# Block 15 sums its products of Q and state in TensorE's transposes, GpSimd makes four of its rows of K times v, and the calls of all engines are in another order

## The chip, the cores and the metric

The kernel runs on one core of one Trainium2 chip. Its time is the device time of one launch in microseconds (us). The kernel before has a median of 511.01 us over three runs (510.86 to 511.65).

## The reference

The input x is 8 sequences of 1024 tokens of 128 features, all float32. One layer is computed: a gated linear recurrence with 16 heads of width 8, then a normalisation, then a feed-forward part of hidden width 512 and a second normalisation. Cut to what matters:

```
q, k, v = x @ Wq, x @ Wk, x @ Wv                 # heads of 8
f = sigmoid(x @ Wf + bf)
state[i, j] = state[i, j] * f[i] + v[i] * k[j]   # for every token, per head
out[i] = sum over j of state[i, j] * q[j]
out = (layernorm(out) * gamma + beta) * silu(x @ Wg)
x1 = layernorm(x + out @ Wout)
h = silu(x1 @ w1 * s1) * (x1 @ w2 * s2)
h = gelu(h @ h1 * sh1);  h = gelu(h @ h2 * sh2)
y = layernorm(x1 + (h @ w3) * s3)
```

## The kernel before, in words

The 8192 tokens are cut into 16 blocks of 512. Every block has the same work, block 0 and the last feed-forward part in forms of their own. Two blocks make one sequence, so the state starts at zero in even blocks and is carried over in odd ones.

**Recurrence.** Features lie on the 128 partitions, tokens along the row. TensorE makes v, f, k, q and the gate from xT (project_v and so on). q and k go out to a buffer in memory and come back so that each of 8 rows j holds, on all partitions of a head, feature j of k (tile KJ) or of q (tile QJ). For each j, K times v is formed, then a scan over the 512 tokens with the forget gate g (scan, L1601). DVE forms K times v two rows at a time (kv, L1585), rows 0 to 5 in most blocks; GpSimd forms rows 6 and 7 one at a time (kv_gp, L550). DVE multiplies Q by the state two rows at a time (qs, L1608). The sum over the 8 rows is then made by three adds of two rows each on DVE (add, L1616), which leave two rows, and one add of one row on GpSimd (add_gp, L556). sum_transposed (L2313) transposes the one row left in 4 chunks of 128 tokens into PSUM bank back. The blocks in the set EARLY, before only block 1, do it otherwise: GpSimd makes rows 4 to 7 of K times v, no adds are done, and sum_transposed accumulates the 8 rows in 32 transposes.

**Rest of the attention.** Statistics on DVE (stats_o), their root on GpSimd (rstd_of), the norm on ScalarE (norm_o), a transpose (transpose_y), scale and shift on ScalarE (affine), the gate on GpSimd (gated_y), the output product (attention_out), the residual on DVE, the statistics and norm of x1, and its transpose (transpose_x1), which ScalarE splits into a high part and DVE into a low part (x1_lo).

**Feed-forward part.** The products run in fp32r, with activations as high plus low part. up_hi and up_lo give the two up-projections in four groups t; ScalarE applies silu and DVE multiplies (hmul, L1665). Two middle layers follow, each with mid_open, mid_hi and mid_lo: the low parts come from GpSimd (lo, L489) and gelu from ScalarE. last_begin and last_rest make the last product and residual_2 adds x1. Block 15's feed-forward part is cut into two halves (tail_ calls).

**Order.** Nothing schedules at run time: each engine has one list of calls written out by hand, and semaphores tie the lists together. TensorE overwrites a PSUM bank only behind the wait that a table FREED names. sum_transposed(n) waits for the sum (in EARLY blocks for all products of Q and state, qs_done) and for residual_2(n-2), which reads bank back. In rest(), up_hi(n, t) with t of 2 or 3 waits for hmul of t-2, and mid_open of layer 1 waits for three hmul at t = 0 and for all four at t = 2. For a while at the start TensorE is given products that nobody reads (keep_busy, L2242). The weights' low parts are summed at the start and a flag tells TensorE which of two program parts to run: count_low_parts (L2485) on TensorE, set_flag (L1724) on DVE, then the load of the flag and a branch.

Of the kernel before, what the change touches and what calls it, by code (L numbers as in the profile page):

```python
# [3 lines left out]
def build_program(nc, x_d, xT_d, wproj_d, wffn_d, w3_d, w3s_d, cols_d, ident_d, out_d):  # L4
# [22 lines left out]
    EARLY = range(1, 2)  # L27
# [10 lines left out]
    with ctx:  # L38
# [213 lines left out]
        def _(e):  # L252
# [84 lines left out]
            send(1, 1)  # L337
            load_w3()
            load_xT(3)
            fetch(1, 1, 0)  # L340
            fetch(1, 1, 1)
            send(1, 0)
            load_weights(3)
            load_x(0)
# [9 lines left out]
            load_x(1)  # L354
            send(3, 0)
            fetch(2, 0, 1)
            fetch(3, 1, 0)
            fetch(3, 1, 1)
            send(4, 1)
            load_x(2)  # L360
            load_x(3)
            load_xT(5)
            fetch(3, 0, 0)
            load_x(4)
            fetch(4, 1, 0)
            load_x(5)
            fetch(3, 0, 1)
            send(4, 0)
            fetch(4, 1, 1)
            fetch(4, 0, 0)  # L370
            fetch(4, 0, 1)
            send(5, 1)
            load_xT(6)
            store(0)
            fetch(5, 1, 0)
            fetch(5, 1, 1)
            send(5, 0)
            fetch(5, 0, 0)
            fetch(5, 0, 1)
            send(6, 1)  # L380
            load_xT(7)
            load_xT(8)
            load_x(6)
            fetch(6, 1, 0)
            fetch(6, 1, 1)
            store(1)
            send(6, 0)
            fetch(6, 0, 0)
            load_xT(9)
            fetch(6, 0, 1)  # L390
            store(2)
            send(7, 1)
            load_x(7)
            load_xT(10)
            send(7, 0)
            fetch(7, 1, 0)
            fetch(7, 1, 1)
            send(8, 1)
            load_x(8)
            fetch(7, 0, 0)  # L400
# [3 lines left out]
            send(8, 0)  # L404
            fetch(8, 0, 0)
            fetch(8, 1, 1)
            load_x(9)
            send(9, 1)
            load_xT(11)
            fetch(8, 0, 1)  # L410
            send(10, 1)
            load_x(10)
            fetch(9, 1, 0)
            send(9, 0)
# [3 lines left out]
            load_xT(12)  # L418
            load_x(11)
            fetch(9, 0, 1)  # L420
            send(10, 0)
            fetch(10, 1, 0)
            fetch(10, 0, 0)
            store(5)
            send(11, 1)
            fetch(10, 0, 1)
            fetch(10, 1, 1)
            fetch(11, 1, 0)
            fetch(11, 1, 1)
            send(11, 0)  # L430
            load_xT(13)
            fetch(11, 0, 0)
            fetch(11, 0, 1)
            store(6)
            send(12, 0)
            load_x(12)
            load_x(13)
            load_xT(14)
            send(12, 1)
            fetch(12, 1, 0)  # L440
            fetch(12, 0, 0)
            store(7)
            fetch(12, 0, 1)
            send(13, 0)
            fetch(12, 1, 1)
            fetch(13, 0, 0)
            send(13, 1)
            load_x(14)
            store(8)
            fetch(13, 1, 0)  # L450
            fetch(13, 1, 1)
            store(9)
            fetch(13, 0, 1)
            load_xT(15)
            send(14, 1)
            fetch(14, 1, 0)
            load_x(15)
            send(14, 0)
            fetch(14, 1, 1)
            send(15, 1)  # L460
            fetch(14, 0, 0)
            fetch(15, 1, 0)
            store(10)
            fetch(14, 0, 1)
            fetch(15, 1, 1)
            send(15, 0)
# [4 lines left out]
            store(13)  # L471
            store_last(1)
            store(14)
# [9 lines left out]
        def _(e):  # L483
# [87 lines left out]
            kvj_gp(4)  # L571
            scale_w3()
            qsj_gp(1)
# [6 lines left out]
            kv_gp(1, 6)  # L580
            rstd_of(0, "1")
            kv_gp(1, 7)
# [19 lines left out]
            lo(1, 1, 2)  # L602
            lo(1, 1, 3)
            gated_y(2)
            rstd_2(0)
            lo(2, 1, 0)
            lo(2, 1, 1)
            rstd_of(2, "1")
            lo(2, 1, 2)
            lo(2, 1, 3)  # L610
            kv_gp(4, 6)
            add_gp(3)
            lo(1, 2, 0)
            lo(1, 2, 1)
# [2636 lines left out]
```

## Time and profile before

| | us |
|---|---|
| median of the runs | 511.01 |
| the profiled execution | 511.23 |
| its span | 509.4 |
| TensorE (PE) busy | 495.7 |
| VectorE (DVE) busy | 447.6 |
| ScalarE (ACT) busy | 404.9 |
| GpSimd (POOL) busy | 311.0 |

The span runs from the first to the last instruction in the trace. Busy times are sums over the span; a matmul's record covers its latency, so a PE that is shown busy can still hold small gaps between the starts of two matmuls. PEld is the loading of weights, which runs beside the matmuls.

### The profile page before, as it was taken

The numbers are of one execution on the slowest core, as the hardware profiler recorded it, in microseconds if no ns is written. First come the engines' busy times: TensorE is split into PE (matmuls) and PEld (weight loads), VectorE is DVE, ScalarE is ACT, GpSimd is POOL, SyncE is SP. The second block draws the span as 40 slices with busy tenths as digits, with TensorE's granted clock in tenths as the row PEclk, the third lists the DMA queues.
The fourth block names the chain that finished last, engine by engine and source line by source line (L and its number), as shares of the span: only waits on it lengthen the run. The fifth ranks groups of instructions, "written<-read, shape, count | busy, mean of one in ns | idle before, by whom it ended". The sixth has DMA issues, their size and how long they took to land. (4 is left out here: it accounts for less than half of the span.)

```text
span 509.4 us, 7961 instructions
## 1 busy us (share of the span) xinstructions
PE 495.7 (97%) x2528; PEld 383.1 (75%) x2528; DVE 447.6 (88%) x708; ACT 404.9 (79%) x839; POOL 311.0 (61%) x362
## 2 busy tenths in 40 slices
PE   9989999999999999999999999999999999999995
PEld 5667787777877777777877777777877777777895
DVE  3999999999989999999899999899999899992352
ACT  5765878787888977888897887889878788868764
POOL 0742839577592838768384775848385784929341
PEclk9999999999999999999999999999999999999999
DMA  7997999935797779768988895905875850700001
GB/s 244 250 269 181 258 257 226 234 87 150 186 264 195 221 178 239 187 164 201 248 210 214 209 257 150 244 2 145 209 181 154 218 126 18 190 1 1 23 2 65
DMA packets 21772, 87.33 MB, mean 171 GB/s; under 512 B 2528, under 2 KB 3552, under 8 KB 13792
## 3 DMA queue, kind: packets, MB, share of 16 engines
q1 hardware_dynamic: 21440, 86.46, 66.9%
q8 instruction: 22, 0.36, 0.3%
q10 hardware_dynamic: 288, 0.33, 0.2%
q14 instruction: 22, 0.18, 0.1%
HBM read 74.72 MB, written 12.06 MB: 170 GB/s over the span
## 5 line engine op out<-in xcount | busy, mean ns | idle before, releaser
L915 ACT ACTIVATE h<-F,cols 128x512 f32<-128x512 f32 x120 | 80.4, 688 | 11.3 <-PE F L2345 10.6
L489 POOL TENSOR_TENSOR h1lo<-h,h1hi 128x512 fp32r<-128x512 f32 x60 | 76.2, 1289 | 11.9 <-ACT h1hi L908 11.8
L489 POOL TENSOR_TENSOR h2lo<-h,h2hi 128x512 fp32r<-128x512 f32 x60 | 76.0, 1288 | 6.7 <-ACT h2hi L908 6.6
L1601 DVE TENSOR_TENSOR_SCAN KJ<-g,carry,KJ 128x512 f32<-128x512 f32 x64 | 78.2, 1262 | 0.0
L2345 PE MATMUL F<-h2hi,whi 128*128 128x512 f32 (+1 forms) x256 | 74.7, 424 | 0.2
L1601 DVE TENSOR_TENSOR_SCAN KJ<-g,KJ 128x512 f32<-128x512 f32 x64 | 74.3, 1203 | 0.7 <-POOL KJ L537 0.4
L1608 DVE TENSOR_TENSOR QJ<-QJ,KJ 128x1024 f32<-128x1024 f32 x60 | 71.2, 1213 | 0.2
L2345 PE MATMUL F<-h1hi,whi 128*128 128x512 f32 (+1 forms) x256 | 68.9, 411 | 2.4 <-DVE h L1665 2.1
L550 POOL TENSOR_TENSOR KJ<-KJ,v_sb 128x512 f32<-128x512 f32 x32 | 42.4, 1332 | 43.9 <-DMA KJ<-qk_bounce 26.9
L2345 PE MATMUL F<-h1lo,whi 128*128 128x512 f32 (+1 forms) x256 | 67.1, 401 | 0.0
L2345 PE MATMUL F<-h2lo,whi 128*128 128x512 f32 (+1 forms) x256 | 65.8, 398 | 0.4 <-POOL h2lo L489 0.3
L2246 PE MATMUL front<-xT,wproj 128*128 128x512 f32 x122 | 63.1, 598 | 0.8 <-ACT gate L855 0.6
L556 POOL TENSOR_TENSOR QJ<-QJ 128x512 f32<-128x512 f32 x14 | 18.0, 1285 | 74.1 <-DVE QJ L1616 74.1
L2345 PEld LDWEIGHTS F<-h1hi,whi 128*128 128x128 f32 x256 | 44.9, 188 | 22.9 <-issue 11.6
L2345 PEld LDWEIGHTS F<-h2hi,whi 128*128 128x128 f32 x256 | 46.9, 188 | 19.9 <-issue 6.7
L2446 PEld LDWEIGHTS back<-w,h 128*128 128x128 f32 x480 | 57.5, 191 | 2.7 <-DVE x1lo L1660 0.5
L2446 PE MATMUL back<-w,h 128*128 128x128 f32 x480 | 58.2, 275 | 0.0
L2345 PEld LDWEIGHTS F<-h1lo,whi 128*128 128x128 f32 x256 | 46.2, 188 | 12.4 <-issue 2.9
L2345 PEld LDWEIGHTS F<-h2lo,whi 128*128 128x128 f32 x256 | 45.7, 188 | 12.2 <-POOL h2lo L489 2.0
L1616 DVE TENSOR_TENSOR QJ<-QJ 128x1024 f32<-128x1024 f32 x42 | 52.3, 1245 | 1.3
L1585 DVE TENSOR_TENSOR KJ<-ps_v,KJ 128x1024 f32<-128x1024 f32 x44 | 52.7, 1207 | 0.0
L902 ACT ACTIVATE h<-F,cols 128x512 f32<-128x512 f32 x60 | 40.0, 685 | 14.3 <-PE F L2345 13.7
(183 smaller groups left out, 934.9 us busy)
## 6 DMA issues: line engine op xcount, KB each, us to landing
KJ<-qk_bounce SPq DMA_DIRECT2D x30, 1024.0 KB, 9.9
QJ<-qk_bounce SPq DMA_DIRECT2D x30, 1024.0 KB, 10.7
qk_bounce<-qk SPq DMA_DIRECT2D x30, 256.0 KB, 4.0
x_in<-in_x SPq DMA_DIRECT2D x16, 256.0 KB, 9.1
xT<-in_xT SPq DMA_DIRECT2D x15, 256.0 KB, 4.9
out<-res SPq DMA_DIRECT2D x15, 256.0 KB, 5.8
wraw<-in_wffn SPq DMA_DIRECT2D x2, 1024.0 KB, 9.4
wraw<-in_wffn SPq DMA_DIRECT2D x2, 256.0 KB, 4.7
```

The lines of the kernel that those rows point to most:

```text
L489: e.tensor_tensor(h_lo[layer][:, t, :w], h[:, t, :w], h_hi[layer][:, t, :w].bitcast(f32), ALU.subtract).then_inc(lo_done[layer], 1)
L550: e.tensor_tensor(K, K, v_sb[:, :WIDTH[n]], ALU.mult).then_inc(kv_gp_done, 1)
L556: e.tensor_tensor(first, first, other, ALU.add).then_inc(add_gp_done, 1)
L902: e.activation(h[:, t, :WIDTH[n]], F[2 * (t % 2)][:, :WIDTH[n]], ACT.Silu, scale=S1[t]).then_inc(silu_done, 1)
L915: e.activation(dst[:, t, :WIDTH[n]], F[t][:, :WIDTH[n]], ACT.Gelu, scale=scale[t]).then_inc(gelu_done[layer], 1)
L1585: e.tensor_tensor(K, vb, K, ALU.mult).then_inc(kv_done, 1)
L1601: e.tensor_tensor_scan(K, g[:, :WIDTH[n]], K, init, ALU.mult, ALU.add).then_inc(scan_done, 1)
L1608: e.tensor_tensor(Q, Q, rows(KJ, n)[:, 2 * p:2 * p + 2, :], ALU.mult).then_inc(qs_done, 1)
L1616: e.tensor_tensor(first, first, other, ALU.add).then_inc(add_done, 1)
L2246: return e.matmul(bank[:, :WIDTH[n]], weights, xT[n % XTB][:, :WIDTH[n]], start=True, stop=True)
L2345: return e.matmul(out, whi[:, cs], part, start=start, stop=stop)
L2446: return e.matmul(back[:, chunk(c)], h3[:, k, chunk(c)], w3[:, k, :], start=k == 0, stop=k == NH - 1)
```

## The change

Block 15 joins the set EARLY. With that, its sum goes into 32 transposes, its three adds on DVE and its add on GpSimd are gone, DVE forms rows 0 to 3 of K times v and GpSimd rows 4 to 7. The functions read this from EARLY. One function gets a wait (save_carry, for the order of two writes of the same tile). All else is order: the lists of SP, GpSimd, ScalarE, DVE and TensorE are written anew, and the table FREED with them.

```diff
-    EARLY = range(1, 2)
+
+    EARLY = (1, 15)
...
             def save_carry(n):
+                if n:
+                    e.wait_ge(carry_done, n)
                 e.wait_ge(scan_done, HD * (n + 1))
...
             kv_gp(14, 7)
-            rstd_of(13, "1")
             lo(2, 12, 1)
             lo(2, 12, 2)
             lo(2, 12, 3)
+            rstd_of(13, "1")
+            add_gp(14)
             rstd_2(11)
-            add_gp(14)
-            kv_gp(15, 6)
             lo(1, 13, 0)
+            lo(1, 13, 1)
             rstd_of(14, "o")
-            lo(1, 13, 1)
+            kv_gp(15, 4)
             lo(1, 13, 2)
             lo(1, 13, 3)
             gated_y(14)
-            kv_gp(15, 7)
+            kv_gp(15, 5)
             lo(2, 13, 0)
             lo(2, 13, 1)
+            rstd_of(14, "1")
             lo(2, 13, 2)
-            rstd_of(14, "1")
             lo(2, 13, 3)
-            add_gp(15)
+            kv_gp(15, 6)
+            kv_gp(15, 7)
             lo(1, 14, 0)
+            rstd_2(12)
+            lo(1, 14, 1)
             rstd_of(15, "o")
-            lo(1, 14, 1)
             lo(1, 14, 2)
+            rstd_2(13)
             lo(1, 14, 3)
             gated_y(15)
-            rstd_2(12)
             lo(2, 14, 0)
             lo(2, 14, 1)
             rstd_of(15, "1")
             lo(2, 14, 2)
             lo(2, 14, 3)
-            rstd_2(13)
```

The first place is the end of DVE's part in block 15. KJ1 and QJ1 are the block's rows, h<-F1 and h<-F3 are the hmul of block 14. Before:

```order
L1585 TENSOR_TENSOR KJ1<-ps_v,KJ1 128x1024
L1601 SCALAR_TENSOR_TENSOR KJ1<-g,carry,KJ1 128x512
L1655 TENSOR_TENSOR x_in2<-back,x_in2 128x512
L1601 SCALAR_TENSOR_TENSOR KJ1<-g,carry,KJ1 128x512
L1620 BN_STATS stats_1<-x_in2 128x6 x4
L1626 BN_AGGR mv_1<-stats_1 128x2 x4
L1601 SCALAR_TENSOR_TENSOR KJ1<-g,carry,KJ1 128x512 x3
L1608 TENSOR_TENSOR QJ1<-QJ1,KJ1 128x1024 x3
L1660 TENSOR_TENSOR x1lo<-back,x1hi 128x512
L1616 TENSOR_TENSOR QJ1<-QJ1 128x1024
L1608 TENSOR_TENSOR QJ1<-QJ1,KJ1 128x1024
L1616 TENSOR_TENSOR QJ1<-QJ1 128x1024 x2
```

And now the same stretch:

```order
L1659 TENSOR_TENSOR x_in2<-back,x_in2 128x512
L1624 BN_STATS stats_1<-x_in2 128x6 x4
L1630 BN_AGGR mv_1<-stats_1 128x2 x4
L1605 SCALAR_TENSOR_TENSOR KJ1<-g,carry,KJ1 128x512 x3
L1664 TENSOR_TENSOR x1lo<-back,x1hi 128x512
L1605 SCALAR_TENSOR_TENSOR KJ1<-g,carry,KJ1 128x512 x2
L1612 TENSOR_TENSOR QJ1<-QJ1,KJ1 128x1024 x3
L1669 SCALAR_TENSOR_TENSOR h<-F1,cols,h 128x512
L1612 TENSOR_TENSOR QJ1<-QJ1,KJ1 128x1024
L1677 TENSOR_TENSOR res1<-back,x1_1 128x512
L1669 SCALAR_TENSOR_TENSOR h<-F3,cols,h 128x512
```

The adds are gone, x1lo moved ahead of the last two scans, and the first hmul moved ahead of the fourth product of Q and state.

The second place is GpSimd around block 15's rows. KJ1<-KJ1,v_sb is a row of K times v, h1lo and h2lo are low parts of block 13. Before:

```order
L550 TENSOR_TENSOR KJ1<-KJ1,v_sb 128x512
L489 TENSOR_TENSOR h1lo<-h,h1hi 128x512
L518 TENSOR_TENSOR rstd_o<-mv_o,eps4 128x4
...
L489 TENSOR_TENSOR h1lo<-h,h1hi 128x512 x3
L562 TENSOR_TENSOR y<-y,gate2 128x512
L550 TENSOR_TENSOR KJ1<-KJ1,v_sb 128x512
L489 TENSOR_TENSOR h2lo<-h,h2hi 128x512 x3
L518 TENSOR_TENSOR rstd_1<-mv_1,eps4 128x4
...
L489 TENSOR_TENSOR h2lo<-h,h2hi 128x512
L556 TENSOR_TENSOR QJ1<-QJ1 128x512
```

And now:

```order
L551 TENSOR_TENSOR KJ1<-KJ1,v_sb 128x512
L490 TENSOR_TENSOR h1lo<-h,h1hi 128x512 x2
L563 TENSOR_TENSOR y<-y,gate2 128x512
L551 TENSOR_TENSOR KJ1<-KJ1,v_sb 128x512
L490 TENSOR_TENSOR h2lo<-h,h2hi 128x512 x2
L519 TENSOR_TENSOR rstd_1<-mv_1,eps4 128x4
...
L490 TENSOR_TENSOR h2lo<-h,h2hi 128x512 x2
L551 TENSOR_TENSOR KJ1<-KJ1,v_sb 128x512 x2
L490 TENSOR_TENSOR h1lo<-h,h1hi 128x512
```

The row that stood ahead of the low parts now stands in their midst, and the last two rows follow all of block 13's low parts.

The third place is TensorE ahead of the branch. The tile F<-ones_col,low_any is count_low_parts, F<-wproj,ident is keep_busy, back<-ident,x_0 is transpose_x1(0). Before:

```order
L2331 MATMUL back<-wproj,y 128x128 x4
L2242 MATMUL F<-wproj,ident 128x128 x10
L2485 MATMUL F<-ones_col,low_any 1x1 x4
L2246 MATMUL front<-xT,wproj 128x512
L2242 MATMUL F<-wproj,ident 128x128 x16
L2230 MATMUL back<-ident,x_0 128x128 x4
L2246 MATMUL front<-xT,wproj 128x512
L2242 MATMUL F<-wproj,ident 128x128
L3205 TENSOR_LOAD flag
```

And now:

```order
L2246 MATMUL ps_v<-xT,wproj 128x512
L2246 MATMUL front<-xT,wproj 128x512
L2331 MATMUL back<-wproj,y 128x128 x4
L2242 MATMUL F<-wproj,ident 128x128 x26
L2230 MATMUL back<-ident,x_0 128x128 x4
L2485 MATMUL F<-ones_col,low_any 1x1 x4
L2242 MATMUL F<-wproj,ident 128x128
L2246 MATMUL front<-xT,wproj 128x512
L3205 TENSOR_LOAD flag
```

The count moved behind transpose_x1(0), the projections moved around it; on DVE, set_flag moved from ahead of half_norm("1") to behind qs(1, 0) and qs(1, 1).

## Rows read from the trace of the kernel before

**Rows 1.** The page: busy time of each engine, and the clock line.

```profile
PE 495.7 (97%) x2528; PEld 383.1 (75%) x2528; DVE 447.6 (88%) x708; ACT 404.9 (79%) x839; POOL 311.0 (61%) x362
...
PEclk9999999999999999999999999999999999999999
```

**Rows 2.** Windows, all engines: stretch, length, busy us and instructions, clock, DMA share, GB/s.

```profile
60.00:420.00 360.00, 357.40 (x1744) 273.72 (x1743) 341.99 (x508) 299.54 (x621) 239.22 (x273) 1.00 0.77 192
420.00:460.00 40.00, 37.83 (x199) 29.57 (x197) 38.89 (x60) 30.98 (x60) 21.68 (x25) 1.00 0.27 67
460.00:509.40 49.40, 43.50 (x304) 39.42 (x302) 15.82 (x58) 33.91 (x82) 22.94 (x31) 0.98 0.07 23
```

**Rows 3.** Waits of PE: us in total, times, longest.

```profile
PE F L2345 <- DVE h L1665: 2.8, 5, 1.1
```

**Rows 4.** Timeline of PE at block 1's sum: start, us, engine, line.

```profile
49.07 3.65 PE L2313 MATMUL back<-ident,QJ 128*128 128x128 f32 x32
```

**Rows 5.** Timelines of PE and PEld around block 15's sum.

```profile
456.89 0.60 PE L2313 MATMUL back<-ident,QJ 128*128 128x128 f32 x4
...
459.62 3.17 PE L2345 MATMUL F<-h1hi,whi 128*128 128x512 f32 x12 [1.14 <-DVE h L1665]
...
455.86 0.30 PEld L2345 LDWEIGHTS F<-x1hi,whi 128*128 128x128 f32 x2 [0.58 <-DVE h L1665]
...
460.18 2.16 PEld L2345 LDWEIGHTS F<-h1hi,whi 128*128 128x128 f32 x10 [0.30 <-DVE h L1665]
```

**Rows 6.** Sources, one line each: ns min/median/max, first and last start.

```profile
L1616 DVE TENSOR_TENSOR QJ<-QJ x42: 1214/1219/2250, 70.7 to 453.9; 128x1024 f32<-128x1024 f32 x42
...
L1585 DVE TENSOR_TENSOR KJ<-ps_v,KJ x44: 1190/1212/1218, 24.5 to 437.6; 128x1024 f32<-128x1024 f32 x44
...
L556 POOL TENSOR_TENSOR QJ<-QJ x14: 1272/1282/1304, 76.1 to 455.2; 128x512 f32<-128x512 f32 x14
...
L550 POOL TENSOR_TENSOR KJ<-KJ,v_sb x32: 1262/1288/2176, 26.8 to 437.2; 128x512 f32<-128x512 f32 x32
...
L902 ACT ACTIVATE h<-F,cols x60: 672/687/691, 44.9 to 458.5; 128x512 f32<-128x512 f32 x60
```

**Rows 7.** Timeline of DVE, end of block 15's part.

```profile
442.82 3.60 DVE L1601 TENSOR_TENSOR_SCAN KJ<-g,carry,KJ 128x512 f32<-128x512 f32 x3
446.34 3.47 DVE L1608 TENSOR_TENSOR QJ<-QJ,KJ 128x1024 f32<-128x1024 f32 x3
...
455.06 0.75 DVE L1665 SCALAR_TENSOR_TENSOR h<-F,cols,h 128x512 f32<-128x512 f32 x1
```

**Rows 8.** Timeline of POOL, 427 to 446 us.

```profile
428.18 1.28 POOL L550 TENSOR_TENSOR KJ<-KJ,v_sb 128x512 f32<-128x512 f32 x1
...
439.05 2.53 POOL L489 TENSOR_TENSOR h2lo<-h,h2hi 128x512 fp32r<-128x512 f32 x2 [0.52 <-ACT h2hi L908]
441.81 1.28 POOL L489 TENSOR_TENSOR h2lo<-h,h2hi 128x512 fp32r<-128x512 f32 x1 [0.23 <-ACT h2hi L908]
...
444.58 1.30 POOL L489 TENSOR_TENSOR h2lo<-h,h2hi 128x512 fp32r<-128x512 f32 x1
```

**Rows 9.** Timelines at the branch: DVE, PE; the flag's load by its source line.

```profile
40.58 0.12 DVE L1724 CAST flag<-F 1x1 int32<-1x1 f32 x1
...
41.14 2.34 DVE L1608 TENSOR_TENSOR QJ<-QJ,KJ 128x1024 f32<-128x1024 f32 x2
...
46.32 1.39 DVE L1665 SCALAR_TENSOR_TENSOR h<-F,cols,h 128x512 f32<-128x512 f32 x2
...
43.50 0.71 PE L2345 MATMUL F<-x1hi,whi 128*128 128x512 f32 x2
...
L3205 PEldq TENSOR_LOAD <-flag x1: 489/489/489, 41.6 to 41.6; - x1
```

**Rows 10.** Timelines of DVE and ACT at the first scan.

```profile
11.45 1.21 DVE L1601 TENSOR_TENSOR_SCAN KJ<-g,KJ 128x512 f32<-128x512 f32 x1
...
9.82 0.60 ACT L847 ACTIVATE g<-th 128x512 f32<-128x512 f32 x1
```

More of the change, by code:

```diff
@@ L1074, in _ @@
             silu(1, 0)
+            silu(1, 1)
             hi(1, 1, 0)
-            silu(1, 1)
-            square(0)
-            silu_gate(3)
-            silu(1, 2)
-            silu(1, 3)
-            hi(1, 1, 1)
-            hi(1, 1, 2)
-            tanh(4)
-            norm_o(2)
-            hi(1, 1, 3)
+            silu(1, 2)
+            hi(1, 1, 1)
+            silu_gate(3)
+            silu(1, 3)
+            hi(1, 1, 2)
+            g_of_tanh(3)
+            hi(1, 1, 3)
+            norm_o(2)
+            square(0)
             affine(2)
@@ L1759, in _ @@
             scan(1, 2)
+            scan(1, 3)
             gated_y0()
-            scan(1, 3)
+            scan(1, 4)
             residual_1(0)
@@ L1771, in _ @@
             qs(1, 1)
+            set_flag()
             x1_lo(0)
@@ L1984, in _ @@
             qs(9, 1)
+            add(9, 0)
             qs(9, 2)
-            add(9, 0)
             x1_lo(8)
@@ L2039, in _ @@
             qs(11, 2)
+            qs(11, 3)
+            x1_lo(10)
             add(11, 0)
-            x1_lo(10)
             add(11, 1)
-            qs(11, 3)
             add(11, 2)
+            hmul(10, 0)
+            residual_2(9)
             kv(12, 0)
-            hmul(10, 0)
             hmul(10, 1)
-            residual_2(9)
-            scan(12, 0)
             hmul(10, 2)
@@ L2052, in _ @@
             hmul(10, 3)
+            scan(12, 0)
+            kv(12, 1)
             scan(12, 1)
-            kv(12, 1)
             scan(12, 2)
@@ L2122, in _ @@
             add(14, 0)
+            x1_lo(13)
+            add(14, 1)
             qs(14, 3)
-            add(14, 1)
             add(14, 2)
             hmul(13, 0)
+            hmul(13, 1)
             residual_2(12)
-            hmul(13, 1)
             stats_o(14)
@@ L2532, in rest @@
                 up_lo(1, 1, low_parts)
-                project_gate(3)
-                sum_transposed(2)
                 up_hi(1, 2, low_parts)
                 up_lo(1, 2, low_parts)
+                sum_transposed(2)
+                project_gate(3)
                 up_hi(1, 3, low_parts)
@@ L2983, in rest @@
                 up_hi(12, 2, low_parts)
+                up_lo(12, 2, low_parts)
+                sum_transposed(13)
                 up_hi(12, 3, low_parts)
-                sum_transposed(13)
-                up_lo(12, 2, low_parts)
                 up_lo(12, 3, low_parts)
@@ L3026, in rest @@
                 up_lo(13, 3, low_parts)
-                project_q(15)
+                project_gate(15)
                 mid_open(1, 13, 0, low_parts)
```

963 lines of the change are left out of this document (478 added, 485 removed).

## The prediction

> **What bounds the kernel now.** I read the page's busy line first [rows 1]: TensorE (PE) is busy for 495.7 of 509.4 us and VectorE (DVE) for 447.6. The reader should see that both are nearly full, and that the TensorE clock is at its upper level in nearly every slice. The windows [rows 2] say where each is full. From 60 to 420 us PE is busy for 357.4 of 360 us, so 2.6 us are idle; from 420 to 460 us 37.83 of 40 (2.17 idle) while DVE has 38.89; after 460 DVE has little to do and PE's 5.9 idle us lie in the last closing steps. So PE sets the pace, DVE is close behind until block 15 is through the scan, and what PE waits for in the whole span is small; the largest is 2.8 for the product of the two up-projections on DVE, h at L1665 [rows 3]. The consequence for any change: work added to PE costs its full length, and work taken from DVE pays only as far as PE was waiting for DVE.
>
> **TensorE's extra transposes.** sum_transposed(15) has had one row to transpose in 4 chunks; it gets 8 rows, 32 transposes, as block 1 has. Block 1's 32 take 3.65 us in a row and block 15's 4 take 0.60 [rows 4, 5]; a transpose's own latency is in both, so the pace is (3.65 - 0.60) / 28 = 0.109 us, and 28 more cost 3.05 us. They stand in the middle of PE's queue, in front of up_hi(14, 3), with the middle layers of block 14 behind them. PE has no hole of that length there: its waits there are the 0.30 to 1.14 us of [rows 5]. I take +3.05. The Trainium skill ("TensorE: Matmul & The Clock Gate", Part 4: PE-mode transpose) gives about 275 ns for a 128x128 transpose in a kernel's context; by it, as an estimate, 28 would be 7.7 us. Row and rule differ, since the row is a pace of transposes that overlap, and the row decides for this chain.
>
> **DVE's relief.** Three adds of 1.22 us and one product of K and v of 1.21 us go [rows 6], 4.9 us of DVE in block 15. GpSimd (POOL) loses one add of 1.28 and makes two more rows of K times v at 1.29 each, 1.3 us net [rows 6]. What PE could get back is what it waits for DVE here: 1.14 us before the middle layer's first products, and up to 0.58 at up_hi(14, 2) [rows 5]. DVE reached that product late because the adds stood ahead of it, to 455.1 [rows 7]. But the adds' place is not simply empty. In the new order the rows 4 to 7 of K times v come from POOL, and rows 6 and 7 stand behind both last low parts of layer 2 of block 13. In the trace the last of those ends at 445.9 [rows 8]. The row that POOL made at 428.18, before the low parts of layer 1 were there, now stands in their midst (1.29 us), of which POOL's two gaps at 439.05 and 441.81 (0.52 and 0.23) take 0.75: the queue is 0.5 late. So row 7 of K times v is ready at about 445.9 + 0.5 + 2 x 1.29 = 449.0. DVE then still has the last scan (1.3 with its start), three products with Q (3.47 in a row), and only then hmul(14, 0): 449.0 + 1.3 + 3.5 = 453.8, against 455.06 before [rows 7]. Of the 4.9 us saved 1.3 arrive; the rest is DVE waiting for POOL and for x1hi, whose use (x1lo) now stands ahead of the last two scans. Behind hmul(14, 0), 0.7, come the fourth product with Q and the residual, 453.8 + 0.7 + 1.2 + 0.7 = 456.4: from then on PE may overwrite back and start the 32 transposes, which take PE 3.5 us, to 459.9. up_hi and up_lo of (14, 3) take 0.9 more, silu 0.7 [rows 6], hmul(14, 3) 0.75 and the passing of signals some 0.1, so h is complete at 462.4, and the third mid_open of layer 1 waits for it. Before, its weights were loaded at 460.18 [rows 5]. By this count PE is 2.2 us later, so 0.85 of the 3.05 comes back. Bounds: 3.5 us late (nothing back, and POOL's queue 0.5 late beside it), and 0.9 late (all of the 2.17 idle us before 460 back).
>
> The other side of moving rows to POOL is that both engines read the same memory. The slowest product of K and v on POOL took 2.18 us against a median of 1.29, and the slowest add on DVE 2.25 against 1.22 [rows 6]; something held each of them up, seldom, and I take it that it was the other engine. The Trainium skill ("SBUF — State Buffer", Who interferes with whom) says that a DVE instruction with two SBUF inputs and a GpSimd one that reads SBUF exclude each other. The scans and K products read one input from PSUM, so the two new rows beside them would cost nothing by the rule either, and taking out adds can only help. I cost this at 0; if one pair collides, 1 us.
>
> **The start.** The flag that says whether low parts of the weights are zero is now counted behind transpose_x1(0), and DVE sets it behind two products with Q. Before, the flag was set at 40.58, the two products ended at 43.48 and PE went on at 43.50 without a gap [rows 9]. In the new order the flag is set no earlier than 43.5, and loading it and the branch, of which the load alone took 0.49 us [rows 9], come after. I put up_hi(0, 0) at 44.5, 1.0 late. DVE has work of its own between, and reached the first hmul at 46.32, 2.8 after PE's first product, so part of the delay is swallowed; I take half: +0.5. Bounds: +1.1 (all of it), and -0.6, because tanh and g now stand ahead of the weights' sums on ScalarE and the first scan can start 0.8 earlier (it began at 11.45 while g was there at 10.42 [rows 10]).
>
> **The other orders.** Loads, projections and norms of blocks 2 to 14 change places with their neighbours, with the same instructions in all. They can take from 2.6 us of idle at most [rows 2], or add as much. Half is my value, -1.3, since one order of this kind should remove some waits that the other has; the bounds are -2.6 and +1.0. One move I looked at in particular: project_q(15) leaves the place just before mid_open(1, 13, 0), and project_gate(15) takes it, so that place is neutral. The DMA calls on SP change places too; from 420 to 460 us, where the end is decided, the DMA engines are busy for 0.27 of their time [rows 2], so I cost that at nothing. A load that came late in the middle would show as a wait of a scan or a product for a DMA, and would be part of the 1.0 us bound.
>
> **Sum.** 511.23 (this execution's time, 509.4 of span and 1.8 around it) + 3.05 - 0.85 + 0.5 - 1.3 = 512.6. The profiled execution is 0.2 over the median of 511.01, so against the median of the runs I forecast 512.4, 0.3% slower. The measurement tells about 0.2% from nothing, 1.0 us: faster is below 510.0, slower above 512.0.
>
> **Rivals.**
> 1. The relief reaches PE. If POOL's rows come as early as DVE asks, all 2.17 idle us of 420 to 460 go, and the middle gives 1.3, the start 0: 511.2 + 3.05 - 2.17 - 1.3 = 510.8, or 510.6 against the median: no change. For it: DVE was full to 455 and PE's largest waits name it [rows 3]. Against it: the rows 6 and 7 stand behind two low parts on POOL.
> 2. Faster, by the orders. The mechanism is PE's idle time in blocks 2 to 14: if the new order takes all 2.6 of it, the start gains 0.6 and the end all of its 2.17, the sum is 511.2 + 3.05 - 2.17 - 2.6 - 0.6 = 508.9, or 508.7. It decides from the point where more than 4.1 us of waits go away, since 3.05 have to be paid first. For it: every call order was written anew, and ScalarE's start is better placed. Against it: PE has hardly 4.8 idle us between 60 and 460, and all would have to go.
> 3. Slower by more. POOL's queue, fuller by a row at 437, delays the low parts and the norm of x1(14), so that PE waits before transpose_x1(14) as well as after the 32 transposes: 1.5 more, 514.1, or 513.9 against the median. For it: the last low part came at 445.9 in a queue with only two gaps behind it. Against it: those two gaps were waits for ScalarE's high parts [rows 8], so there ScalarE was late, not POOL.
> 4. By the skill's 275 ns a transpose the time would be about 4.6 us (7.7 - 3.05) over my sum, 517.0; block 1's row, at 0.109 a piece, leaves it 1 in 100, and it is counted with rival 3.
>
> **Chances.** Forecast (slower by 0.7 to 2.7 us) 0.50; rival 1 0.24; rival 2 0.18; rival 3 with 4 0.08. The forecast's low edge falls into no change for 0.05 of its 0.50, so faster 0.18, same 0.29, slower 0.53. The range reaches from inside rival 2 to rival 3: 509.8 to 514.7, leaving out about 1 in 10 on the fast side and less on the slow side. The forecast's own range is 511.7 to 513.7.
>
> **What would show it.** L2313 has 116 transposes, and one run of 32 near 457 that takes 3.65 us. L1616 falls to 39 and DVE's busy time by about 4.9. DVE shows idle time before a scan of block 15, released by K rows of POOL, and before x1lo; if it shows none and hmul(14, 0) comes before 452, the second step is wrong and rival 1 holds. PE's wait for h at the first middle products of block 14 is still 1 us or more. At the start the flag is set near 43.6 and PE has a gap of about 1 us before x1hi's first product; if the first product comes by 43.5, that step is wrong. Between 60 and 420 PE's idle should be 1 to 2 us; under 0.5 speaks for rival 2, over 3.6 breaks my bound.

## The result, and the profile after

The changed kernel takes 512.26 us (median; 511.64 to 513.88 over 12 runs) against 510.89 (509.73 to 511.77, 12 runs). The ratio is 1.0029, 95% interval 1.0019 to 1.0039: slower by 1.4 us, and the forecast was 512.4. The total came out right; the steps did not all, as the sections below show.

The page of the profiled execution (511.81 us, of which 510.0 of span), busy time per engine, and its clock line:

```profile
PE 499.0 (98%) x2556; PEld 386.5 (76%) x2556; DVE 444.0 (87%) x704; ACT 405.3 (79%) x839; POOL 312.9 (61%) x363
...
PEclk9999999999999999999999999999999999999999
```

TensorE (PE) has 28 instructions and 3.3 us more than in [rows 1], VectorE (DVE) 3.6 us less, and the granted clock is at its upper level throughout. The windows of the kernel after, with the columns of [rows 2]:

```profile
60.00:420.00 360.00, 358.66 (x1747) 274.30 (x1746) 342.98 (x509) 298.02 (x617) 238.68 (x271) 1.00 0.76 187
420.00:460.00 40.00, 38.53 (x222) 31.74 (x221) 32.99 (x47) 32.89 (x65) 24.15 (x28) 1.00 0.38 94
460.00:510.00 50.00, 45.20 (x314) 40.77 (x312) 17.98 (x66) 34.28 (x82) 22.87 (x31) 0.98 0.07 23
```

From 60 to 420 us PE is idle for 1.34 us instead of 2.60, and from 420 to 460 for 1.47 instead of 2.17, while DVE falls from 38.89 us of work to 32.99 there. Around block 15's sum, the timeline of PE (start, us, engine, line; in brackets the idle time before, and what ended it):

```profile
456.92 3.65 PE L2313 MATMUL back<-ident,QJ 128*128 128x128 f32 x32
460.33 0.71 PE L2345 MATMUL F<-x1hi,whi 128*128 128x512 f32 x2
...
463.06 1.20 PE L2345 MATMUL F<-h1hi,whi 128*128 128x512 f32 x4 [1.10 <-DVE h L1669]
```

The sum starts at 456.92, within 0.03 us of where it was [rows 5], takes 3.65 us as block 1's does [rows 4], and the same 1.1 us of waiting for h follows. From there the marks that I compared are 2.7 to 2.9 us later, down to the last products. DVE in the same stretch:

```profile
447.66 0.69 DVE L1664 TENSOR_TENSOR x1lo<-back,x1hi 128x512 fp32r<-128x512 f32 x1 [1.52 <-ACT x1hi L899]
448.31 2.53 DVE L1605 TENSOR_TENSOR_SCAN KJ<-g,carry,KJ 128x512 f32<-128x512 f32 x2
450.76 3.47 DVE L1612 TENSOR_TENSOR QJ<-QJ,KJ 128x1024 f32<-128x1024 f32 x3
454.15 0.74 DVE L1669 SCALAR_TENSOR_TENSOR h<-F,cols,h 128x512 f32<-128x512 f32 x1
```

DVE stands idle for 1.52 us ahead of x1lo, and reaches h of (14, 0) at 454.15, where it was 455.06 [rows 7]. POOL, whose two rows of K times v the last scans need:

```profile
444.48 2.54 POOL L490 TENSOR_TENSOR h2lo<-h,h2hi 128x512 fp32r<-128x512 f32 x2
446.97 2.56 POOL L551 TENSOR_TENSOR KJ<-KJ,v_sb 128x512 f32<-128x512 f32 x2
```

The second row is ready at 449.5 and the last scan begins at 449.6. At the branch, PE's first product of the first FFN block has moved from 43.50 [rows 9] to 45.12:

```profile
45.12 0.72 PE L2345 MATMUL F<-x1hi,whi 128*128 128x512 f32 x2 [0.60 <-issue]
```

What the forecast had not looked at is the close. The last products in the kernel before, then the issues of its last stores by SyncE's queue (out<-QJ is store_last, out<-res at 504.34 is store(14)):

```profile
501.46 2.11 PE L2477 MATMUL F<-w,h 128*128 128x128 f32 x16
```

```profile
503.91 0.39 SPq L312 DMA_DIRECT2D out<-QJ  x1
504.34 0.46 SPq L302 DMA_DIRECT2D out<-res  x1
504.85 0.94 SPq L312 DMA_DIRECT2D out<-QJ  x2
```

The same in the kernel after (x3: store_last 1 to 3; out<-res is store(14)):

```profile
504.26 2.11 PE L2477 MATMUL F<-w,h 128*128 128x128 f32 x16
```

```profile
501.03 0.33 SPq L303 DMA_DIRECT2D out<-res  x1
505.54 2.81 SPq L313 DMA_DIRECT2D out<-QJ  x3
```

The last product ends at 506.37 where it was 503.57, but the span grew by only 0.6 us: from the last product to the end it takes 3.64 us instead of 5.86. Before, norm_2(14) stood behind the tail's last gelus and store(14), 256 KB, was issued at 504.34, in between the last small stores. So the two profiled executions differ by +2.8 at the last product and by -2.2 behind it. What those 2.2 us are is under the run that moves store(14) alone, below.

### The profile page after: what moved, and what is told of

It is laid out like the page before. It is cut to its first block, busy times and chain, and to the rows that moved or that the text cites. A ratio compares the mean times of both kernels' runs of the same rounds, so it can differ in the third digit from the quotient of the medians.

```text
span 510.0 us, 8027 instructions
## 1 busy us (share of the span) xinstructions
PE 499.0 (98%) x2556; PEld 386.5 (76%) x2556; DVE 444.0 (87%) x704; ACT 405.3 (79%) x839; POOL 312.9 (61%) x363
## 4 chain that ended last, share of the span: by engine, by line
PE 85%; ACT 6%; POOL 5%; issue 3%; DVE 1%; POOLq 0%; ACTq 0%
PE F L2345 50%; PE back L2446 10%; PE front L2246 8%; PE back L2230 3%; PE back L2331 3%; PE back L2313 2%; PE ps_v L2246 2%; POOL h2lo L490 1%; PE F L2242 1%; POOL h1lo L490 1%; ACT h L919 1%; PE F L2237 1%; ACT h L906 1%; PE F L2246 1%; DVE h L1669 1%
## 5 line engine op out<-in xcount | busy, mean ns | idle before, releaser
L2345 PE MATMUL F<-h2hi,whi 128*128 128x512 f32 (+1 forms) x256 | 72.2, 418 | 0.2
L2345 PE MATMUL F<-h1lo,whi 128*128 128x512 f32 (+1 forms) x256 | 65.1, 396 | 0.0
L551 POOL TENSOR_TENSOR KJ<-KJ,v_sb 128x512 f32<-128x512 f32 x34 | 44.5, 1317 | 33.4 <-DMA KJ<-qk_bounce 25.8
L2345 PEld LDWEIGHTS F<-h1hi,whi 128*128 128x128 f32 x256 | 45.1, 188 | 23.3 <-issue 10.6
L557 POOL TENSOR_TENSOR QJ<-QJ 128x512 f32<-128x512 f32 x13 | 16.8, 1290 | 58.2 <-DVE QJ L1620 58.2
L1669 DVE SCALAR_TENSOR_TENSOR h<-F,cols,h 128x512 f32<-128x512 f32 x60 | 44.1, 745 | 5.3 <-ACT h L906 4.6
```

Source lines behind the costliest of these rows:

```text
L551: e.tensor_tensor(K, K, v_sb[:, :WIDTH[n]], ALU.mult).then_inc(kv_gp_done, 1)
L557: e.tensor_tensor(first, first, other, ALU.add).then_inc(add_gp_done, 1)
L1669: e.scalar_tensor_tensor(h[:, t, :w], F[2 * (t % 2) + 1][:, :w], S2[t], h[:, t, :w], ALU.mult, ALU.mult).then_inc(hmul_done, 1)
L2345: return e.matmul(out, whi[:, cs], part, start=start, stop=stop)
```

## Experiments

Every ratio is to runs of the kernel before on the same chip (medians 510.7 to 511.1); two kernels that were run on different chips are compared by their ratios, times 511 us. "Product to end" is the stretch from the last product to the end of the span in the profiled execution.

| kernel | median us (range) | ratio, 95% interval |
|---|---|---|
| before + early close | 508.59 (508.0-509.2) | 0.9959 [0.9943, 0.9975] |
| after + old close | 515.88 (514.9-517.1) | 1.0097 [1.0080, 1.0114] |
| after, 4 transposes | 512.13 (510.7-514.1) | 1.0034 [1.0016, 1.0051] |
| after, early flag | 512.63 (511.6-513.8; one launch of 1756.7 left out) | 1.0037 [1.0025, 1.0049] |
| before + block 15's edit alone | 518.93 (518.0-520.2) | 1.0161 [1.0139, 1.0184] |
| after with block 15's old sum | 514.73 (513.4-518.0) | 1.0071 [1.0052, 1.0090] |
| before + block 15's edit + early close | 516.89 (515.7-518.0) | 1.0121 [1.0099, 1.0142] |
| after, store(14) behind store_last(1) | 514.30 (512.6-515.8) | 1.0073 [1.0048, 1.0097] |
| before to 440 us, then after | 510.94 (509.9-513.6) | 1.0006 [0.9992, 1.0019] |
| after to 440 us, then before | 514.02 (512.2-517.1) | 1.0068 [1.0043, 1.0092] |
| before + early close, 28 more transposes | 511.78 (510.8-514.0) | 1.0015 [1.0003, 1.0027] |
| before to 440, then after, 4 transposes | 511.24 (508.6-513.6) | 1.0011 [0.9992, 1.0029] |

**The close, put into the kernel before.** On ScalarE norm_2(13) and norm_2(14) go up into the tail's gelus, on SyncE store(14) ahead of store_last(1):

```diff
 tail_gelu(1, 0, 2)
+norm_2(13)
...
 tail_gelu(2, 0, 3)
+norm_2(14)
 tail_gelu(2, 1, 0)
-norm_2(13)
...
 tail_gelu(2, 1, 3)
-norm_2(14)
...
+store(14)
 store_last(1)
-store(14)
```

> The kernel before, with only its end in the new order: norm_2(13) and norm_2(14) stand further ahead in ScalarE's list and store(14) stands ahead of the last block's own stores. Theory A: the end after the last matmul falls from 5.9 us to about 3.7, since the 256 KB of store(14) no longer go out among the last stores; time 2.0 to 2.2 us below before, PE's marks up to 500 us unchanged. Rival B: the shorter end of the changed kernel comes from something else (the order of the tail's products); then this one is within 0.3 us of before.

508.59, 0.9959: 2.1 us below the kernel before, from three moved calls. The last product ends at 503.39, 0.2 from where it was, and product to end is 3.7 us instead of 5.9. The early close is a gain of its own, worth all of the 2.1 us, and this version beats both kernels. (Theory A's reason, the 256 KB among the last stores, is looked at under the third run.)

**The old close, put into the kernel after.** The same edit backwards.

> The changed kernel with norm_2(13), norm_2(14) and store(14) back in the old places. Theory A: 2.0 to 2.2 us slower than the changed kernel, 3.4 to 3.6 over before; the last matmul ends where it did (506.4 after the span's start) and 5.8 us follow. Rival B: within 0.3 us of the changed kernel.

515.88, by the ratios 3.5 us over the kernel after where 2.2 were expected. Product to end is back at 5.87 us, so 2.2 of it are the close. The profiled execution (517.05, the longest of its five) has another 2.9 us ahead of the last product, and they begin in block 9, far from the edit; what happened there is in the last section.

**Which half of the close.** Only SyncE's order goes back; norm_2(14) stays early.

```diff
-store(14)
 store_last(1)
+store(14)
```

> The changed kernel with one order of the DMA queue of SyncE back: store(14) behind store_last(1), norm_2(14) stays early in ScalarE's order. Theory A (the 256 KB store just ahead of the last two small stores is what made the end after the last matmul 5.9 us long): the store now waits behind store_last(1) whatever ScalarE does, so 512.3 + 2.0 = 514.3, and 5.9 us from the last matmul to the end. Rival (ScalarE's late norm_2(14) was the cause, the place on the queue is nothing): 512.3 and 3.6 us. The run with both orders back gave 515.9, of which 2.9 us in its trace lay ahead of the last matmul: if this run has that too, it comes with the queue's order; if not, with ScalarE's.

The median is the 514.3 that theory A gave, and still the profile refutes it. Product to end is 3.87 us, not 5.9:

```profile
506.52 0.39 SPq L313 DMA_DIRECT2D out<-QJ  x1
506.96 1.60 SPq L303 DMA_DIRECT2D out<-res  x1
508.60 0.93 SPq L313 DMA_DIRECT2D out<-QJ  x2
```

The large store is again between the small ones, and the end is hardly longer: in the profiled execution the place on the queue costs 0.2 us. So 256 KB between the small stores do not by themselves make the end long.

The traces show what does: the very last store, 64 KB. From issue to landing it took 3.6 us in the kernel before and 1.6 in the kernel before with the early close; the small store ahead of it took 1.9 and 1.6. In the kernel before its last nine packets run only after a packet of 16 KB of the queue that the profile calls instruction (q8) has ended. Stretches 506.9 to 507.9 and 507.9 to 508.5 (queue: packets, MB, share of 16 engines; 5.9% is one engine):

```profile
q8 instruction: 1, 0.02, 5.9%
```

```profile
q1 hardware_dynamic: 9, 0.00, 5.9%
```

With the early close all of the store's packets are through before such a packet begins. Stretches 506.0 to 506.25 and 506.25 to 507.2:

```profile
q1 hardware_dynamic: 87, 0.04, 51.2%
```

```profile
q8 instruction: 1, 0.02, 6.2%
```

This goes through all fourteen profiles. Nine packets run after the 16 KB one in five, and product to end is 5.5 to 5.9 us there; in the other nine it is 3.6 to 3.9. The five are the three kernels with the old close, and two with the early close, "after, early flag" (5.8) and "after with block 15's old sum" (5.5). So neither order decides it alone. In those two the 16 KB packet begins 2.75 us after the last product, where in the short ends the store's packets are through at 2.83 to 3.04. How often the packet gets in the way in each kernel is not known beyond one profile per kernel, nor is what starts it; why the old close met it three times out of three stays open. The times of the kernel before with the early close, 508.0 to 509.2 in all six launches, suggest that there it was seldom or never met.

By the ratios this kernel is 2.2 us over the kernel after. Of that 1.0 lies ahead of the last product in the profile and is again the drift from block 9. The profiled execution, 513.02, is 1.3 below the median, so what the longer launches had is not seen.

**Four transposes in the kernel after.**

```diff
-terms = HD if n in EARLY else 1
+terms = HD if n == 1 else 1
```

> The changed kernel with 4 transposes for block 15 and not 32: seven of the eight rows of the sum of block 15 are left out, all else stays. Theory A (work added to PE costs its length): 2.8 to 3.1 us faster than the changed kernel, 1.4 to 1.8 below before. Rival C (the 1.10 us wait behind the transposes is there anyway, set by the chain through stats_o and norm_o): the same, since that chain is shorter too. Rival D (the 28 are partly hidden): less than 2 us faster.

512.13: no gain in the median. The profiled execution (511.06) reached block 15's first tail product 0.85 us earlier than the kernel after. Most of what the transposes leave turns into waits of PE:

```profile
457.02 0.60 PE L2313 MATMUL back<-ident,QJ 128*128 128x128 f32 x4
457.82 0.73 PE L2345 MATMUL F<-x1hi,whi 128*128 128x512 f32 x2 [0.21 <-DVE h L1669]
...
459.49 0.71 PE L2345 MATMUL F<-h1hi,whi 128*128 128x512 f32 x2 [0.48 <-DVE h L1669]
461.43 2.59 PE L2345 MATMUL F<-h1hi,whi 128*128 128x512 f32 x10 [1.23 <-DVE h L1669]
464.65 0.63 PE L2230 MATMUL back<-ident,o_norm 128*128 128x128 f32 x4 [0.63 <-ACT o_norm L864]
```

The clock stayed at its upper level in this execution. The twelve launches differ in it: the five with a mean granted clock of 0.999 or 1.000 have a median of 511.06, the seven with 0.994 to 0.998 one of 513.06. So the 0.85 us of the trace seem to be there where the clock holds, and to be lost where it falls; no launch with a lower clock was profiled.

**The flag back ahead of the products.** VectorE's set_flag() before half_norm("1"), TensorE's count_low_parts() back ahead of keep_busy(16).

> The changed kernel with the flag counted and set where the kernel before does it. Theory A: PE's first product of x1hi comes at 43.9 to 44.2 and not 45.12 us; by block 5 both orders stand at the same time, since DVE and PE have slack to take it up, so the total is within 0.4 us of the changed kernel. Rival E: the start is carried to the end, 1.0 to 1.6 us faster than the changed kernel.

512.63, not faster. In its trace PE's first product comes 0.7 us earlier than in the kernel after, and from block 2 on both run together, within 0.2 us. That delay at the start is swallowed. (The profiled execution, 513.81, is the longest of the eight; its last product comes 0.1 us before that of the kernel after, and the rest is the long close described above.)

**Block 15's edit alone, and with the early close.** The kernel before with EARLY = (1, 15), GpSimd's rows 4 to 7 and VectorE's four instructions out; all else stays. The second has the early close too.

```diff
-EARLY = range(1, 2)
+EARLY = (1, 15)
...
-kv(15, 2)
...
-add(15, 0)
-add(15, 1)
-add(15, 2)
```

> The kernel before with block 15's part of the change alone: 32 transposes instead of 4, GpSimd makes rows 4 to 7 of K times v, VectorE loses kv(15,2) and its three adds; every other order is as before, the old close of the program too. Theory A (the summing on TensorE costs what block 15's stretch showed, +2.8 us, less the little that four transposes in the changed kernel gave back): 510.7 + 2.0 to 3.0 = 512.7 to 513.7, the last matmul that much later than 503.6, and the end after it still 5.9 us. Theory B (alone, most of it hides behind waits for VectorE, as the run with four transposes suggests: 0.85 us of difference in its trace): 511.3 to 511.9. Theory C (VectorE's relief outweighs it): at most 510.7.

> The kernel before with block 15's part of the change and with norm_2(13), norm_2(14) and store(14) early; the flag, the loads and the middle are as before. Theory A (pieces add): the first run of this call plus the close's -2.1; against the kernel before 510.7 + 2.8 - 2.1 = 511.4, range 510.6 to 512.0. Theory B (block 15's part alone is mostly hidden): 509.2 to 509.9. If it equals the kernel after (512.3), the rest of the orders is worth nothing; where it stands below it by over 0.5 us, the start or the middle costs that.

518.93 and 516.89: 8 and 6 us slower, far outside every theory; their difference is the close again, 2.0 us. The reason is an order I had left alone. Timeline of DVE in the first of the two, then of PE:

```profile
446.87 2.54 DVE L1602 TENSOR_TENSOR_SCAN KJ<-g,carry,KJ 128x512 f32<-128x512 f32 x2 [3.33 <-POOL KJ L550]
449.32 3.47 DVE L1609 TENSOR_TENSOR QJ<-QJ,KJ 128x1024 f32<-128x1024 f32 x3
452.71 0.68 DVE L1661 TENSOR_TENSOR x1lo<-back,x1hi 128x512 fp32r<-128x512 f32 x1
```

```profile
453.45 1.44 PE L2443 MATMUL back<-w,h 128*128 128x128 f32 x6 [3.00 <-DVE x1lo L1661]
```

The last two scans wait 3.33 us for POOL's rows, and x1lo of block 14 is queued behind them and three products; PE waits 3.00 us for it. In the changed kernel x1_lo(14) stands ahead of those two scans. The wait is shown; that moving x1_lo(14) alone would remove it was not run, and the kernels below move the whole end. And the wait costs more than its length, as the windows behind it show (clock in the third column from the right):

```profile
452.00:454.00 2.00, 0.55 (x3) 0.56 (x4) 2.00 (x3) 0.11 (x1) 0.00 (x0) 0.93 0.00 0
454.00:456.00 2.00, 2.00 (x10) 1.81 (x9) 0.52 (x1) 0.22 (x1) 0.00 (x0) 0.50 0.00 0
456.00:458.00 2.00, 2.00 (x15) 2.00 (x15) 0.75 (x1) 0.47 (x1) 0.00 (x0) 0.72 0.00 0
```

After the idle stretch PE is granted 0.50, that is 1.2 GHz, and comes back to 2.4 GHz only within the third window.

**The new orders with the old sum.** The kernel after with EARLY = range(1, 2), VectorE's adds and kv(15, 2) back, GpSimd's rows 6 and 7 and its add back.

> The changed kernel with block 15 as in the kernel before (4 transposes there, rows 6 and 7 of K times v and the sums by GpSimd and VectorE at their old places), all the other new orders kept: late flag, new loads, new middle, norm_2(14) and store(14) early. Theory A (the pieces add: the start is swallowed, the close gives 2.1): 510.7 - 2.1 = 508.6, range 508.0 to 509.4, and the kernel after is 3 us longer than it. Theory B (the new orders of the middle cost something that shows only at the end): 510.0 to 511.0.

514.73, by the ratios 2.1 us slower than the kernel after; the expectation was 3 us faster. Here VectorE has its 4.9 us back, and in the profiled execution (517.95, the longest of seven) h of (14, 0) is ready only at 461.4; the timeline of PE, then its windows:

```profile
461.46 1.22 PE L2348 MATMUL F<-x1hi,whi 128*128 128x512 f32 x2 [3.40 <-DVE h L1668]
```

```profile
460.00:462.00 2.00, 0.54 (x1) 0.50 (x2) 2.00 (x4) 0.56 (x2) 1.18 (x1) 0.79 0.00 0
462.00:464.00 2.00, 2.00 (x8) 1.56 (x7) 0.66 (x2) 0.98 (x3) 1.87 (x4) 0.50 0.00 0
```

PE waits 3.40 us and the clock falls to half behind it. This execution is not a typical one: its span is 6.1 us over that of the kernel after, of which 1.9 are there at block 14's first product already (the drift from block 9), 2.3 more by the last product, and 1.8 are the long close. The granted clock averaged over a run was 0.995 to 0.997 in all seven, against 0.997 to 1.000 in the kernel after.

**The program cut at 440 us.** Since the three runs above suggest that block 15's edit and its neighbours' order belong together, the next two exchange the whole end. On every engine the calls up to block 15's part are of the one kernel, and those behind it of the other, always with the early close. (In the first, x1_hi(14) is also moved ahead of gelu(2, 13, 0), as after has it.)

> Every engine's calls as in the kernel before up to about 440 us, and from block 15's K times v on exactly as in the kernel after: the 32 transposes, GpSimd's rows 4 to 7, x1_lo(14) ahead of the last two scans, the new tail, norm_2(14) and store(14) early. What it lacks of the change is the start and the middle. Theory A (start and middle cancel, so that all of the change's time is made in the last 70 us: +2.8 in block 15, -2.2 at the close): 512.0 to 512.6, the same as the kernel after, with x1hi of block 15 at 477.0 + 2.2 to 2.9. Theory B (block 15's part was tuned together with the middle ahead of it, as the run with block 15's part alone at +8 suggests): 514 to 518. Theory C (the start's 1.6 us are not all swallowed): 510.8 to 511.6.

> The other way round: the kernel after up to about 440 us, and from there the kernel before with norm_2(14) and store(14) early (the order that gave 508.6). 4 transposes in block 15, VectorE's three adds and kv(15,2), x1_lo(14) behind three products of Q. Theory A (start and middle cancel): 508.3 to 509.2, equal to the kernel before with the early close, and so 3.5 us below the kernel after: that is then the price of block 15's part. Theory B (the middle leaves VectorE later than before had it, which only block 15's relief makes good): 511 to 515; the run with the new orders and the old sum at 514.7 speaks for it.

The first: 510.94, 1.0006. Against the kernel before with the early close this is +0.0047, 2.4 us: the price of block 15's part, whole. Against the kernel after it is -0.0023, 1.2 us: what the new start and middle cost, where theory A had them cancel (the two intervals just touch at 1.0019, so this size is loose). In its trace the sum begins earlier by what VectorE's relief gives:

```profile
455.84 3.66 PE L2310 MATMUL back<-ident,QJ 128*128 128x128 f32 x32
...
461.99 2.60 PE L2342 MATMUL F<-h1hi,whi 128*128 128x512 f32 x10 [1.10 <-DVE h L1666]
```

With the early close alone the sum began at 456.6, so 0.8 us come back ahead of it; block 15's first tail product is 2.1 us later than there. The seam also brings the new order of the tail with it, so this price is that of the part and its new neighbours together.

The second, 514.02, settles less than I wanted. In its profile PE waits once for 2.1 us for ScalarE's copy of Q and K: at the seam TensorE already runs in the new order and ScalarE's copy_q(15) still stands in the old one. That wait is of my making, and no price of block 15's part can be read from this run.

**28 more transposes and nothing else.** The kernel before with the early close; each of block 15's four transposes is made eight times, each a start of its own.

```diff
-terms = HD if n in EARLY else 1
+terms = HD if n in (1, 15) else 1
...
-rows(QJ, n)[:, j, chunk(c)] ... start=j == 0, stop=j == terms - 1)
+rows(QJ, n)[:, 0 if n == 15 else j, chunk(c)] ... start=j == 0 or n == 15, stop=j == terms - 1 or n == 15)
```

> The kernel before with the early close (508.6) and, in block 15's sum, each of the four transposes made eight times over, each a start of its own, so that the value is that of the last: 28 transposes more on TensorE and nothing else touched, VectorE's adds stay. Theory A (a transpose costs its 0.109 us of TensorE and all of it arrives): 508.6 + 3.05 = 511.7. Theory B (waits behind it, 1.1 us for h in block 14's middle products, take up part of it, and VectorE's later free moment is not needed): 508.6 + 1.9 to 2.2 = 510.5 to 510.8. Theory C (as the run with four transposes in the changed kernel had it, 0 to 0.9): 508.6 to 509.5.

511.78, +0.0056 or 2.9 us over the kernel before with the early close (508.59). From block 14's first product to block 15's first tail product the trace is 3.05 us longer than there (at block 14's first product it is 0.6 late already, 0.4 of it from before block 0's first product). Theory A: the whole 3.05 arrives. The wait of PE behind it did not shrink:

```profile
457.21 3.66 PE L2313 MATMUL back<-ident,QJ 128*128 128x128 f32 x32
...
462.99 3.17 PE L2345 MATMUL F<-h1hi,whi 128*128 128x512 f32 x12 [1.20 <-DVE h L1665]
```

It was 1.14 [rows 5]. In that order VectorE has hmul(14, 2) and hmul(14, 3) behind stats_o(15), and stats_o(15) waits for the transposes: the h that PE waits for moves along with them.

**The same transposes taken out of the new end.** The kernel cut at 440 us, with row 0 alone in block 15's sum.

> The kernel that follows the kernel before up to about 440 us and the kernel after from there (510.9), with block 15's sum made of row 0 alone: 4 transposes, so that rows 1 to 7 of Q times state are left out of block 15's result. Everything else, VectorE's relief and x1_lo(14) ahead of the last two scans, stays. Theory A (the 28 transposes cost their 3.05 us, as they did in the kernel with nothing else changed, and VectorE's relief is worth 0.85): 510.9 - 3.05 = 507.9, below the kernel before with the early close (508.6). Theory B (with the new order of VectorE its products of h, not TensorE, set the pace behind the sum, so that the time of the transposes is hidden under the waits, as the same cut in the changed kernel gave -0.85 in its trace and nothing in its median): 510.0 to 510.9, with waits for h of 2 us or more on TensorE between 456 and 465 us.

511.24, no gain over 510.94, though the fastest of twelve took 508.62. So the 3 us that arrive in full in one order do not come back in the other, and the profile shows two reasons. PE's timeline, then its windows:

```profile
455.89 0.60 PE L2310 MATMUL back<-ident,QJ 128*128 128x128 f32 x4
456.70 0.73 PE L2342 MATMUL F<-x1hi,whi 128*128 128x512 f32 x2 [0.21 <-DVE h L1666]
...
458.38 0.70 PE L2342 MATMUL F<-h1hi,whi 128*128 128x512 f32 x2 [0.49 <-DVE h L1666]
460.31 3.93 PE L2342 MATMUL F<-h1hi,whi 128*128 128x512 f32 x10 [1.24 <-DVE h L1666]
```

```profile
456.00:460.00 4.00, 2.38 (x11) 1.22 (x9) 3.06 (x11) 3.70 (x11) 3.47 (x4) 1.00 0.00 0
460.00:464.00 4.00, 3.69 (x10) 2.81 (x11) 0.26 (x1) 2.66 (x10) 3.84 (x8) 0.65 0.00 0
```

PE now waits for h three times, 1.9 us in all instead of 1.1, so the ten products begin only 1.7 us earlier than behind 32 transposes; and having been idle for 1.6 of 4 us PE is granted 0.65 in the next 4, so they take 3.93 us instead of 2.60. The clock did not fall in the execution with four transposes in the kernel after, though its waits were nearly the same; so this is what can follow such waits, not what must. In the twelve runs the mean clock was 0.994 to 0.999, with a median of 0.997, against 0.997 to 1.000 with 32 transposes. An estimate from that: a mean of 0.997 over 511 us is some 1.5 us lost at half clock, one of 0.995 some 2.6 us; with the 0.8 us of longer waits that is most of what the missing transposes could have given.

## Why the prediction was right in total and wrong in steps

The steps beside what the runs gave (us; measured sizes are differences of ratios times 511, or of traces where two values stand; by their intervals each is good to about 1 us):

| step | forecast | measured | from |
|---|---|---|---|
| 28 transposes | +3.05 | +2.9 | 28 more transposes alone |
| VectorE's relief | -0.85 | -0.5 to -0.9 | the cut at 440 us against it |
| start and middle | +0.5 - 1.3 = -0.8 | about +1.2 | kernel after against the cut |
| close | 0 | -2.1 | early close in the kernel before |
| sum | +1.4 | +1.5 | |

The measured steps are a chain of kernels from the one before to the one after, so that they add up to the total says nothing about their sizes.

**The transposes.** Right: 116 transposes at L2313, 32 of them in 3.65 us, and 28 alone cost 2.9 us. The estimate of 7.7 us from the Trainium skill's 275 ns ("TensorE: Matmul & The Clock Gate", Part 4) does not hold here: 275 ns is how long one lasts (the trace has 273), not the pace in a row of 32. What the term hid is that it holds only for the order it was put into. "PE has no hole of that length there" is true of the kernel before; in the new order the waits for h, and the clock where it falls behind them, take up the time once the transposes are gone.

**The relief.** Right in size and by its mechanism. POOL's row 7 was due at 449.0 and came at 449.5; hmul(14, 0) at 453.8 and came at 454.15; the third opening of block 14's middle layer at 462.4 and its products came at 463.06. DVE's idle time ahead of x1lo is there, as said. The mark before a scan is not: x1hi, not POOL, was the later of the two by the trace. DVE's busy time fell by 3.6, not 4.9, though the four instructions are gone (L1620, the adds, has 39). Taken alone, the adds have 4.7 us less (1.0 of it a long add near 279.5 in the kernel before only) and K times v 1.0 less. But an instruction often begins some 0.1 us before the end of the one ahead of it, and such a stretch is counted once; with DVE idle in between, fewer stretches are: the products of h count 0.7 us more.

**Start.** The place was right, and in this pair the size too small: the first product came at 45.12, not 44.5, and is 1.6 late, above my bound of 1.1. The traces scatter here, though: over all profiles it came at 43.5 to 44.2 where the start is the old one (seven, median 43.9) and at 44.4 to 45.5 with the new start (six, median 45.1), so 1.2 late by the medians. The delay is gone at block 5's first product in the trace. The run with the early flag, 0.7 us sooner at that product, gains nothing. So "part is swallowed" was too weak: all of it is, as far as this run reaches.

**Middle.** This step failed. Idle time did go down as forecast, by 1.3 us, and I counted that as time. But at the first products of blocks 8 to 13 the changed kernel stands between -1.1 and +2.2 us from the kernel before, at block 14's +0.6, and the cut at 440 us, with the old start and middle, is 1.2 us faster. Less idle time in a fixed window means nothing when a kernel has reached another point of its program by then. What in the middle costs it was not taken apart.

**Close.** Not in the forecast at all. I had read "PE's 5.9 idle us lie in the last closing steps" and treated them as fixed. The change moves norm_2(13), norm_2(14) and store(14) there, and this is its only clear gain; in the traces all of it is the landing of the last store. That the total fits to 0.1 us is luck: +2.0 of error in the middle and start against -2.1 at the close.

Rivals 1 and 3 fell. The relief did not reach PE beyond 0.9; 1.1 us of waiting for h is where it was. Rival 2's place, the orders, did hold a gain of 2.1, but at the end of the program and not in blocks 2 to 14.

## What to carry to other kernels

Put a price on an edit only together with the order that it stands in. Block 15's sum on TensorE cost 8 us with its neighbours left alone, 2.4 us with them moved, and taking its transposes out again gained nothing; where VectorE was the late one, the same part was worth 2.1 us (1.0071 against 1.0029). And read what comes after the last product as well as the middle: there three moved calls gave 2.1 us. Look at each store's landing by itself: here one store of 64 KB made the whole difference.

## What was not expected of the hardware

**The clock.** A wait of some 3 us, or several waits that left PE idle 1.6 of 4 us, was followed by 2 to 4 us at a granted clock of 0.50 to 0.72, with products of 128x512 at 0.43 us apart instead of 0.23. So in this kernel a wait costs up to twice its length (1.9 us of waits and 1.3 more for the ten products behind them), and work that merely fills such a gap cost nothing. In the other profiled executions waits of 1.0 to 1.2 us left the clock at 1.00, and so did the one of 2.1 us at the seam. And once, with four transposes in the kernel after, waits like those that halved it elsewhere left it at 1.00.

**VectorE against GpSimd.** In block 9 an add of VectorE, with two inputs in SBUF, and GpSimd's product of K and v can fall on the same moment. Two kernels with the same order there, first the kernel after, then the one with only store(14) moved:

```profile
278.75 2.55 DVE L1620 TENSOR_TENSOR QJ<-QJ 128x1024 f32<-128x1024 f32 x2
281.29 1.28 POOL L551 TENSOR_TENSOR KJ<-KJ,v_sb 128x512 f32<-128x512 f32 x1 [7.99 <-DMA KJ<-qk_bounce]
```

```profile
278.74 3.44 DVE L1620 TENSOR_TENSOR QJ<-QJ 128x1024 f32<-128x1024 f32 x2
279.23 1.87 POOL L551 TENSOR_TENSOR KJ<-KJ,v_sb 128x512 f32<-128x512 f32 x1 [5.92 <-DMA KJ<-qk_bounce]
```

GpSimd's product starts when a DMA lands. Where it landed 2 us later, two adds took 2.55 us and nothing met; where it landed at 279.2, they took 3.44, everything behind them on VectorE came 0.9 late, and PE 0.8. The drift "from block 9" in the run with the old close has the same long add at 280.4 and another at 369.2. This is the kind of collision that I had costed at 0, or at 1 us if a pair collides. Block 15's own new rows met none in the kernel after (1.29 to 1.31 us each). The one in block 9 was there before the change: the long add stands near 280 in five of the seven profiles with the old middle, and in three of the seven with the new one. So it belongs to an execution, not to an edit, and it is a likely part of why runs of one kernel spread over 2 us and of what the runs with the old orders at the close and with block 15's old sum had too much. One profile per kernel does not say how often it strikes in each, so the medians' share of it stays open.
